# Expert gate and up by halves in three passes, 13 more experts' weights loaded ahead, and the orders at the start and at a seam, in a two-layer transformer kernel

## The chip, the core and the metric

The kernel runs on one core of a Trainium2 chip. A core has TensorE (PE in the profile: matrix products; PEld is its weight load, which overlaps the products), VectorE (DVE), ScalarE (ACT), GpSimd (POOL) and SyncE (SP, which here only issues transfers); 16 DMA engines move data between the chip's memory and the core's on-chip memory. The metric is device time in microseconds (us) of one execution; lower is better. Each engine works through its own list of instructions in order and waits on semaphores where another engine's result is needed.

## The reference, cut to what matters

Two layers act on x of 4 x 256 tokens of width 256 (T = 1024 tokens). All of it is float32.

```
h = layernorm(x) * (1 + ca) + sa                      # layer 0, modulated by a small network on c
x = x + ga * attention0(h)                            # 16 heads, 4-tap causal, gated
h = layernorm(x) * (1 + cb) + sb
x = x + gb * ffn0(h)                                  # silu(h Wg) * (h Wu), Wd; weights decoded from a 16-entry table
h = layernorm(x) * (1 + ca) + sa                      # layer 1
x = x + ga * attention1(h)                            # 16 heads, softmax, mxfp4 weights
h = layernorm(x) * (1 + cb) + sb
x = x + gb * (h + routed(rmsnorm(h)) + shared(rmsnorm(h)))
# routed: each token picks 4 of 32 experts; an expert holds up to 256 tokens:
#   g, u = split(rows @ w13[e]);  rows_out = (silu(g) * u) @ w2[e]
```

## The kernel before

**Layout.** x_t and h_t hold the activations transposed: 128 partitions, two chunks (KC = 2) of 1024 token columns. `psum` is eight banks of 512 float32 columns. `arena` is one large on-chip tile that the phases carve up anew, and `G` another (16 heads x 1024 columns for the attention outputs, then the decoded feed-forward weights). The r forms (`arena_r`, `G_r`) are the same bytes in the type fp32r: a value is rounded to that type when it is written.

**Two ways of multiplying.** A plain float32 product takes two matmul instructions in the trace. The other way is by_halves (lines 641 to 646): each operand is kept as a rounded upper half and the remainder as a lower half, both fp32r, and three matmuls (lower x upper, upper x lower, upper x upper) add into one bank. ACT writes the upper half by a copy, and DVE the lower half by subtracting the upper from the source. Before the change the q, k, z, v projections of layer 0 and the scores and most projections of layer 1 go by halves; the experts do not.

**Start.** The first layernorm runs in two halves of 512 columns, n0a and n0b: mean on PE (L286), subtraction on DVE (L309), squares on ACT (L304), variance on PE (L293), a small TENSOR_SCALAR on DVE (L313), the power -1/2 on POOL (L318), a diagonal of it on DVE (L323), its spreading over partitions by a matmul (L299), then scaling (L329) and modulation (L335) on DVE. The first part of the modulation (`modulation`, PE L622, DVE L1388 and L1393) gives the factors of L335. ACT copies h_t to its upper half (L1224), DVE subtracts (L1419), and the first q projection (L644) waits for that.

**Seam of the two halves of layer 0.** After the heads, PE adds up the output projection (`project_out`, L687: 2 halves n of the tokens x 2 chunks m x 16 heads, one product each), while ACT and DVE decode the feed-forward weights from the table in 13 pieces (`lut_act` L1145 and L1149, `lut_dve` L1487 and L1499). The heads' mean square (r0) comes back from the chip's memory; DVE turns it into a diagonal (L1614), PE spreads it (`spread_pe`, L273), ACT copies it out (L1232), and `attn_half` on DVE (L1583, then L400) uses it. Then come the second norm (n1a, n1b) and the feed-forward (`gate_up` L816, `down` L825). A gate or up product of 512 columns needs a free psum bank: `ffn_bank`.

**Experts.** Before them PE does the layer-1 output projection, DVE the routing (lines 1770 to 1831), and POOL scatters the token rows to `slot_rows` in the chip's memory (32 indirect transfers, L2001). SP loads them back per expert into a ring of 6 (xb, L574), and the weights of an expert (768 columns: 512 of gate and up, 256 of down) into a ring of 4 (L570, then L601). For expert e, PE turns the rows (`turn_rows`, L1041, 4 transposes into bank e % 2), multiplies by gate and up (`up_e`, L1052, 4 products of 256 columns) and by down (`down_e`, L1062). ACT (even e) or DVE (odd e) copies the turned rows out (L1353, L1861), ACT takes silu of the gate (L1359), DVE multiplies with up (L1868), and DVE (even e) or ACT (odd e) copies the output to eo (L1892, L1373). POOL scatters it to `out_rows` by two indirect transfers (L2009), whose targets DVE has copied out (place, L1854). The order is written out by hand: in round e PE does turn_rows(e+2), up_e(e+1), down_e(e). At the end the four chosen rows of each token are read back, weighted and added (o4, in G).

Semaphores of layer 0 are used again in the experts (`REUSED`), so that waits show the old names: a0_q is moe_T, a0_S moe_up_1, a0_A moe_act, a0_vT moe_down, a0_g and a0_gT moe_eo.

## Time and profile before

| what | value |
|---|---|
| median of 3 runs | 1089.62 us (1087.21 to 1091.27) |
| the profiled execution, its own time | 1090.9 us, span on the core 1089.1 us |
| busy share of the span | PE 93%, PEld 74%, DVE 69%, ACT 51%, POOL 26% |
| mean granted TensorE clock | 0.959 |
| start, up to the first q projection | 0 to 27.4 us |
| experts, first turned row to last product | 963.2 to 1062.5 us |

The page gives one row per engine group with its busy time, the mean of one and the idle time before it. The chain of waits follows the work that ended last back from the end; its pieces are laid end to end, so that a piece of eight matmuls divided by eight is the pace of one. The timeline has the same instructions with their full duration: a matmul there shows its own latency, longer than its pace. The granted clock is 1.00 at TensorE's 2.4 GHz level and 0.50 at 1.2 GHz.

### The profile page before, as it was taken

To read this page: it belongs to the slowest core of one execution; us is meant where nothing else is said; L and a number is where in the kernel's file an instruction comes from. 1 tells how busy PE (TensorE), PEld (TensorE's weight loads), DVE (VectorE), ACT (ScalarE), POOL (GpSimd) and SP (SyncE) were. 2 spreads that over 40 slices of the span, in tenths; PEclk is the share of its full clock that TensorE was granted. 3 is DMA by queue.
4 is the path that set the end of the run, shared out by engine and by line. 5 is a ranking of instruction groups with operands and counts; after the bars stand their busy time and mean duration, and the time that the engine had idled before them with its cause. 6 is when DMAs were issued, how large, how long until landed. Compare 5 with 4: busy or idle time off the path is not lost.

```text
span 1089.1 us, 16889 instructions
## 1 busy us (share of the span) xinstructions
PE 1009.2 (93%) x5736; PEld 802.2 (74%) x5736; DVE 751.7 (69%) x1305; ACT 557.8 (51%) x1105; POOL 284.8 (26%) x246
## 2 busy tenths in 40 slices
PE   6979999999999999999979999999996997669996
PEld 4778998898899854354459989889895455358885
DVE  4778999899989859972377777878775144624434
ACT  2558878787887787721155555655552022113231
POOL 1034324423432410030112122121200005436661
PEclk9989999999999999989989999999998998689997
DMA  7087867877876950340011110111002002169956
GB/s 225 3 217 153 190 147 161 169 171 157 166 159 158 259 110 19 133 109 0 1 59 51 37 58 29 58 44 43 29 0 73 0 1 87 57 201 272 274 180 207
DMA packets 82477, 121.56 MB, mean 112 GB/s; under 512 B 26099, under 2 KB 59646, under 8 KB 81792
## 3 DMA queue, kind: packets, MB, share of 16 engines
q1 hardware_dynamic: 70400, 86.88, 26.8%
q0 software_dynamic: 12032, 34.11, 15.9%
q8 instruction: 25, 0.41, 0.2%
q14 instruction: 20, 0.16, 0.0%
HBM read 70.28 MB, written 38.04 MB: 99 GB/s over the span
## 4 chain that ended last, share of the span: by engine, by line
PE 79%; DVE 11%; DMA 3%; ACT 3%; issue 3%; POOL 1%; SPq 0%; ACTq 0%; DVEq 0%; POOLq 0%
PE psum L644 10%; PE psum L646 9%; PE psum L645 9%; PE psum L1052 5%; PE psum L869 5%; PE psum L698 5%; PE psum L1011 5%; PE psum L816 4%; PE psum L894 3%; PE psum L776 3%; PE psum L757 3%; PE psum L1062 2%; PE psum L687 2%; PE psum L825 2%; DVE arena L1511 2%
## 5 line engine op out<-in xcount | busy, mean ns | idle before, releaser
L1511 DVE SCALAR_TENSOR_TENSOR arena<-arena,par_in 128x1024 f32<-128x1024 f32 x144 | 183.5, 1283 | 32.8 <-ACT arena L1136 23.2
L644 PE MATMUL psum<-G_r,arena_r 128*128 128x512 f32 x320 | 132.6, 414 | 7.2 <-DVE G_r L1604 4.1
L645 PE MATMUL psum<-G_r,arena_r 128*128 128x512 f32 x320 | 127.5, 399 | 0.0
L646 PE MATMUL psum<-G_r,arena_r 128*128 128x512 f32 x320 | 127.4, 398 | 0.0
L1960 POOL DMA_DIRECT2D arena<-arena x64 | 53.8, 984 | 210.8 <-DVE arena L1523 210.6
L1284 ACT ACTIVATE arena<-psum,small 128x256 f32<-128x256 f32 x128 | 59.4, 474 | 86.9 <-DVE small L1669 86.9
L1126 ACT ACTIVATE arena<-psum 128x1024 f32<-128x1024 f32 x48 | 49.3, 1027 | 62.2 <-PE psum L646 61.6
L644 PE MATMUL psum<-arena_r 128*128 128x256 f32 x256 | 77.7, 304 | 2.2 <-DVE arena_r L1694 1.5
L644 PEld LDWEIGHTS psum<-G_r,arena_r 128*128 128x128 f32 x320 | 61.2, 191 | 21.2 <-DVE G_r L1604 4.9
L1976 POOL TENSOR_TENSOR arena_r<-arena,arena_r 128x512 fp32r<-128x512 f32 x16 | 20.7, 1294 | 214.2 <-ACT arena_r L1253 214.2
L2009 POOL DMA_INDIRECT out_rows<-arena x64 | 62.6, 979 | 46.8 <-DVE arena L1854 24.5
L645 PE MATMUL psum<-arena_r 128*128 128x256 f32 x256 | 73.4, 287 | 0.0
L646 PE MATMUL psum<-arena_r 128*128 128x256 f32 x256 | 73.3, 286 | 0.0
L646 PEld LDWEIGHTS psum<-G_r,arena_r 128*128 128x128 f32 x320 | 60.8, 190 | 14.8
L645 PEld LDWEIGHTS psum<-G_r,arena_r 128*128 128x128 f32 x320 | 61.3, 192 | 11.4 <-issue 0.2
L2001 POOL DMA_INDIRECT slot_rows<-arena x32 | 31.3, 980 | 128.1 <-issue 111.7
L698 PE MATMUL psum<-cst,arena 128*128 128x128 f32 x512 | 63.9, 278 | 0.0
L869 PE MATMUL psum<-arena,h_t 128*128 128x128 f32 x512 | 62.3, 275 | 0.0
L698 PEld LDWEIGHTS psum<-cst,arena 128*128 128x128 f32 x512 | 59.7, 191 | 3.4 <-issue 3.3
L869 PEld LDWEIGHTS psum<-arena,h_t 128*128 128x128 f32 x512 | 60.9, 192 | 1.5
L1052 PE MATMUL psum<-arena 128*128 128x256 f32 x256 | 61.7, 385 | 0.0
L1136 ACT ACTIVATE arena<-arena,par_in 128x1024 f32<-128x1024 f32 x48 | 55.4, 1154 | 5.5
(243 smaller groups left out, 2375.3 us busy)
## 6 DMA issues: line engine op xcount, KB each, us to landing
arena<-arena POOLq DMA_DIRECT2D x64, 256.0 KB, 5.7
arena<-in_w_moe SPq DMA_DIRECT2D x33, 384.0 KB, 3.9
slot_rows<-nowhere SPq DMA_DIRECT2D x16, 576.0 KB, 4.4
arena<-slot_rows SPq DMA_DIRECT2D x32, 288.0 KB, 4.1
arena<-bands SPq DMA_DIRECT2D x16, 528.0 KB, 4.2
sq_rows<-arena POOLq DMA_DIRECT2D x16, 512.0 KB, 7.5
arena<-in_w_qkvz SPq DMA_DIRECT2D x16, 384.0 KB, 3.8
arena<-in_qkv_codes SPq DMA_DIRECT2D x16, 384.0 KB, 3.2
```

The source lines that it names most:

```text
L644: nc.tensor.matmul(dst, w_l, x_h, start=start, stop=False, skip_group_check=True)
L645: nc.tensor.matmul(dst, w_h, x_l, start=False, stop=False, skip_group_check=True)
L646: return nc.tensor.matmul(dst, w_h, x_h, start=False, stop=stop, skip_group_check=True)
L698: m = nc.tensor.matmul(bank(7)[:, n:n + P], sqr[s][:, i * P:i * P + P], ones, start=True, stop=True, skip_group_check=True)
L869: i = nc.tensor.matmul(dst[:, t * P:t * P + P], h_t[:, k * T + t * P:k * T + t * P + P], w1[par][:, (2 * KC + k) * P:(2 * KC + k) * P + P] ...
L1011: i = nc.tensor.matmul(bank(2 * m + n), wo_c[:, h * D + m * P:h * D + m * P + P], G[:, (OS + h) * T + n * 512:(OS + h) * T + n * 512 + 512 ...
L1052: i = nc.tensor.matmul(bank(2 + 2 * (e % 2) + j)[:, 0:CAP], we[e % WRING][:, k * D + j * P:k * D + j * P + P], xT[e % 2][:, k * CAP:(k + 1 ...
L1136: nc.scalar.activation(by_batch(dst), by_batch(u[s])[:, :, 0:S], ACT.Copy, scale=par_in[:, bass.ds(M_CW + (w * H + h) * TAPS, 1)]).then_in ...
L1284: e = nc.scalar.activation(prob[b % 2][:, i * S:i * S + S], bank(4 + b % 2)[:, i * S:i * S + S], ACT.Exp, bias=nmax[:, 2 * b + i:2 * b + i ...
L1511: nc.vector.scalar_tensor_tensor(by_batch(dst), by_batch(u[s])[:, :, j:j + S], par_in[:, bass.ds(M_CW + (w * H + h) * TAPS + j, 1)], by_ba ...
L1960: nc.gpsimd.dma_start(rot[s][to:to + 64, :], sw[s][of:of + 64, :], accum_op=ALU.add)\
L2009: nc.gpsimd.indirect_dma_start(out_rows, bass.IndirectOffsetOnAxis(place.bitcast(I32)[:, c:c + 1], 0), eo[e % RING][:, r * D:(r + 1) * D], ...
```

## The change

**Experts.** Gate and up go by halves. The turned rows of every expert are copied by ACT to an upper half x_h and subtracted by DVE to a lower half x_l; the gate and up weights likewise to w_h and w_l (2 buffers each). So ACT makes 2 copies of 128x512 per expert where it made one for every other expert, and DVE 2 subtractions of 128x512 where it made one copy for every other expert. PE waits in up_e for w_lo and x_lo. `down_e` stays as it is.

**Weights.** After all of layer 1's output projection has been added up, SP loads experts 4 to 16 at once into the tile G that held the attention outputs. Only 15 experts (17 to 31) are loaded inside the rounds, by the table LATE.

**Start.** PE does the variances before the first modulation; DVE does the split of the first weights (lower0) before the first diagonal, and scales the second half and splits the first before it modulates the second half.

**Seam.** PE spreads r0 five products later. The gate and up of the second piece of the first half (n, m) = (0, 1) go to banks 6 and 7, so that the wait for attn_half(1) moves from that piece (s == 1) to s == 3.

```diff
+AHEAD = 13
+LATE = {1: 27, 3: 28, 5: 29, 7: 17, 8: 18, 10: 19, 11: 20, 13: 21, 14: 22, 16: 23, 17: 24, 19: 25, 20: 26, 22: 30, 24: 31}
...
+        e_halves = carve(*[2 * CAP] * 4, *[2 * D] * 4, base=at_x + NT * TOPK + 2 * E, of=arena_r)
+        x_h, x_l, w_h, w_l = e_halves[0:2], e_halves[2:4], e_halves[4:6], e_halves[6:8]
...
+        w_ahead = carve_g(EW + 4 * T, *[EW] * AHEAD)
...
+            return e - 10 if e < 27 else e - 27
...
-        def ffn_bank(m, up):
+        def ffn_bank(n, m, up):
-            return bank(((0, 3), (1, 2))[m % 2][up])
+            return bank((6, 7)[up] if (n, m) == (0, 1) else ((0, 3), (1, 2))[m % 2][up])
...
+            sp.wait_ge(sg("attn_out"), 4 * KC)
+            for e in range(WRING, WRING + AHEAD):
+                sp.dma_start(we_of(e), a["w_moe"][e]).then_inc(sg("moe_ahead"), 16)
...
-                    if e + WRING < E:
-                        sp.wait_ge(*at("moe_down", e + 1))
-                        sp.dma_start(we[e % WRING], a["w_moe"][e + WRING]).then_inc(sg(f"moe_w{e % WRING}"), 16)
+                    if e in LATE:
+                        late, r = LATE[e], LATE_NTH[LATE[e]] % WRING
+                        sp.wait_ge(*at("moe_down", before(late) + 1))
+                        sp.wait_ge(sg(f"moe_w{r}"), 16 * (LATE_NTH[late] // WRING + 1))
+                        sp.dma_start(we_of(late), a["w_moe"][late]).then_inc(sg(f"moe_w{r}"), 16)
...
-            spread_pe(pe, "r0", fb)
...
-            project_out(1, 0, range(0, 5))
+            project_out(1, 0, range(0, 2))
+            spread_pe(pe, "r0", fb)
+            project_out(1, 0, range(2, 5))
...
-                    if s == 1:
+                    if s == 3:
                         pe.wait_ge(sg("y"), KC + up + 1)
...
             def up_e(e):
-                pe.wait_ge(*at(f"moe_w{e % WRING}", 16 * (e // WRING + 1)))
-                pe.wait_ge(*at(f"moe_xT_{e % 2}", e // 2 + 1))
+                pe.wait_ge(*at("moe_w_lo", e + 1))
+                pe.wait_ge(*at("moe_x_lo", e + 1))
...
-                        i = nc.tensor.matmul(bank(2 + 2 * (e % 2) + j)[:, 0:CAP],
-                                             we[e % WRING][:, k * D + j * P:k * D + j * P + P],
-                                             xT[e % 2][:, k * CAP:(k + 1) * CAP], start=(k == 0), stop=(k == KC - 1))
+                        w, c = slice(k * D + j * P, k * D + j * P + P), slice(k * CAP, (k + 1) * CAP)
+                        i = by_halves(bank(2 + 2 * (e % 2) + j)[:, 0:CAP], w_h[e % 2][:, w], w_l[e % 2][:, w],
+                                      x_h[e % 2][:, c], x_l[e % 2][:, c], k == 0, k == KC - 1)
...
+            def weights_e(e):
+                act.wait_ge(*weights_in(e))
+                if e >= 2:
+                    act.wait_ge(*at("moe_up_1", e - 1))
+                nc.scalar.activation(w_h[e % 2], we_of(e)[:, 0:2 * D], ACT.Copy).then_inc(sg("moe_w_hi"), 1)
...
+            weights_e(0)
+            weights_e(1)
             rows_e(0)
+            rows_e(1)
             silu_e(0)
             for e in range(E):
-                if e % 2 == 0 and e + 2 < E:
+                if e + 2 < E:
                     rows_e(e + 2)
+                    weights_e(e + 2)
...
-                nc.vector.tensor_copy(xT[1], bank(1)).then_inc(sg("moe_xT_1"), 1)
+                nc.vector.tensor_tensor(x_l[e % 2], bank(e % 2), x_h[e % 2].bitcast(F32), ALU.subtract).then_inc(sg("moe_x_lo"), 1)
+
+            def weights_e(e):
+                dve.wait_ge(*at("moe_w_hi", e + 1))
+                if e >= 2:
+                    dve.wait_ge(*at("moe_up_1", e - 1))
+                nc.vector.tensor_tensor(w_l[e % 2], we_of(e)[:, 0:2 * D], w_h[e % 2].bitcast(F32), ALU.subtract)\
+                    .then_inc(sg("moe_w_lo"), 1)
...
                 if e + 2 < E:
+                    rows_e(e + 2)
+                    weights_e(e + 2)
                     place_e(e + 2)
-                if e % 2 and e + 2 < E:
-                    rows_e(e + 2)
```

The list of DVE from its first subtraction, before (L313 the statistic, L323 the diagonal, L1413 lower0, L329 scaling, L335 modulation, L1388 and L1393 the first modulation):

```order
4 L309 TENSOR_TENSOR arena<-x_t,psum 128x512
5 L1388 COPY small<-psum 128x16 [waits mod_ps]
6 L1393 TENSOR_SCALAR small<-small 128x8 [waits mod]
7 L313 TENSOR_SCALAR small<-psum 128x4 [waits norm_var,mod]
8 L323 TENSOR_TENSOR arena<-cst,small 128x512 [waits norm_rstd]
9 L313 TENSOR_SCALAR small<-psum 128x4 [waits norm_var]
10 L323 TENSOR_TENSOR arena<-cst,small 128x512 [waits norm_rstd]
11 L1413 TENSOR_TENSOR arena_r<-arena,arena_r 128x768 [waits a0_w_hi]
12 L329 TENSOR_TENSOR arena<-arena,psum 128x512 [waits norm_spread]
```

The same stretch of DVE after the change (L342 is the statistic, L1464 lower0, L352 the diagonal, L358 scaling, L1439 and L1444 the modulation):

```order
4 L338 TENSOR_TENSOR arena<-x_t,psum 128x512
5 L342 TENSOR_SCALAR small<-psum 128x4 [waits norm_var]
6 L1464 TENSOR_TENSOR arena_r<-arena,arena_r 128x768 [waits a0_w_hi]
7 L352 TENSOR_TENSOR arena<-cst,small 128x512 [waits norm_rstd]
8 L342 TENSOR_SCALAR small<-psum 128x4 [waits norm_var]
9 L352 TENSOR_TENSOR arena<-cst,small 128x512 [waits norm_rstd]
10 L358 TENSOR_TENSOR arena<-arena,psum 128x512 [waits norm_spread]
11 L358 TENSOR_TENSOR arena<-arena,psum 128x512
12 L1439 COPY small<-psum 128x16 [waits mod_ps]
```

The statistic no longer stands behind the modulation, and lower0 stands where DVE waits for POOL's power.

PE at the seam, before (L687 output projection, L273 the spread of r0, L342 the mean of n1a):

```order
626 L687 MATMUL psum<-G,arena 128x512 [waits a0_v_tok]
627 L687 MATMUL psum<-G,arena 128x512 x13
628 L273 MATMUL psum<-arena,cst 128x512 [waits norm_diag,a0_gT_sb]
629 L273 MATMUL psum<-arena,cst 128x512
630 L687 MATMUL psum<-G,arena 128x512 x3
631 L687 MATMUL psum<-G,arena 128x512 [waits a0_on]
632 L687 MATMUL psum<-G,arena 128x512 x4
633 L342 MATMUL psum<-x_t,cst 128x512 [waits x_new] x2
```

PE at the seam after the change (L727, L302 and L377 are the same three):

```order
628 L727 MATMUL psum<-G,arena 128x512 x13
629 L727 MATMUL psum<-G,arena 128x512 [waits a0_gT_sb]
630 L727 MATMUL psum<-G,arena 128x512 x2
631 L727 MATMUL psum<-G,arena 128x512 [waits a0_on]
632 L727 MATMUL psum<-G,arena 128x512
633 L302 MATMUL psum<-arena,cst 128x512 [waits norm_diag]
634 L302 MATMUL psum<-arena,cst 128x512
635 L727 MATMUL psum<-G,arena 128x512 x3
636 L377 MATMUL psum<-x_t,cst 128x512 [waits x_new] x2
```

Five products now stand ahead of the wait for the diagonal (norm_diag).

DVE in two rounds of the experts, before (L1854 place, L1861 turned rows, L1868 silu times up, L1892 output copy):

```order
748 L1854 COPY arena<-arena 128x2 [waits moe_xb0]
749 L1868 TENSOR_TENSOR arena<-psum,arena 128x256 [waits a0_vT,a0_o,a0_S]
750 L1892 COPY arena<-psum 128x512 [waits moe_sc4,moe_over0,a0_vT]
751 L1854 COPY arena<-arena 128x2 [waits moe_xb1]
752 L1861 COPY arena<-psum 128x512 [waits a0_S,a0_q]
753 L1868 TENSOR_TENSOR arena<-psum,arena 128x256 [waits a0_vT,a0_o,a0_S]
```

DVE in two rounds after the change (L1914 is x_lo, which waits for a0_k = moe_x_hi; L1920 w_lo, which waits for a0_ssq = moe_w_hi; L1907, L1928, L1948, L1955 are place, product, one of eight additions of y0 to x_t, output copy):

```order
734 L1914 TENSOR_TENSOR arena_r<-psum,arena_r 128x512 [waits a0_S,a0_k]
735 L1920 TENSOR_TENSOR arena_r<-G,arena_r 128x512 [waits a0_S,a0_ssq]
736 L1907 COPY arena<-arena 128x2 [waits moe_xb4]
737 L1928 TENSOR_TENSOR arena<-psum,arena 128x256 [waits a0_vT,a0_o,a0_S]
738 L1948 SCALAR_TENSOR_TENSOR x_t<-G,small,x_t 128x256
739 L1955 COPY arena<-psum 128x512 [waits moe_sc2,moe_over0,a0_vT]
740 L1914 TENSOR_TENSOR arena_r<-psum,arena_r 128x512 [waits a0_S,a0_k]
741 L1920 TENSOR_TENSOR arena_r<-G,arena_r 128x512 [waits a0_S,a0_ssq]
```

Every round now begins with two subtractions of 128x512, each behind a copy of ACT. On PE a round has 12 fp32r matmuls of 256 columns (L684 to L686) where 4 float32 products stood (L1052, 8 instructions in the trace), between the same transposes and the same down products.

## Rows read from the trace of the kernel before

**Rows 1.** The page: busy time, share and instructions of each engine.

```profile
PE 1009.2 (93%) x5736; PEld 802.2 (74%) x5736; DVE 751.7 (69%) x1305; ACT 557.8 (51%) x1105; POOL 284.8 (26%) x246
```

**Rows 2.** Chain of waits, one expert round: start, us, engine and line.

```profile
986.29 0.44 PE psum L1041 x4
986.73 1.73 PE psum L1052 x8
988.46 0.86 PE psum L1062 x4
```

**Rows 3.** Chain, layer 1: the pace of fp32r matmuls of 256 columns.

```profile
667.39 0.12 PE psum L644
667.51 0.12 PE psum L645
```

**Rows 4.** Windows: PE, PEld, DVE, ACT, POOL busy (count), clock, DMA share, GB/s.

```profile
910.00:920.00 10.00, 5.96 (x33) 4.93 (x31) 3.53 (x8) 2.84 (x6) 7.56 (x9) 0.80 0.31 112
983.00:1003.00 20.00, 20.00 (x108) 17.63 (x107) 10.83 (x28) 5.78 (x13) 13.00 (x13) 1.00 0.90 268
```

**Rows 5.** Timeline, one expert round, ACT and DVE: start, duration, instruction, idle before.

```profile
986.82 0.59 ACT L1353 ACTIVATE arena<-psum 128x512 f32<-128x512 f32 x1
987.63 0.38 ACT L1359 ACTIVATE arena<-psum 128x256 f32<-128x256 f32 x1 [0.22 <-PE psum L1052]
988.50 0.42 DVE L1868 TENSOR_TENSOR arena<-psum,arena 128x256 f32<-128x256 f32 x1 [2.13 <-PE psum L1052]
989.36 0.69 DVE L1892 COPY arena<-psum 128x512 f32<-128x512 f32 x1
```

**Rows 6.** Timeline, POOL's scatters beside a DVE instruction with two on-chip inputs.

```profile
997.93 0.97 POOL L2009 DMA_INDIRECT out_rows<-arena  x1 [1.71 <-issue]
999.20 0.98 POOL L2009 DMA_INDIRECT out_rows<-arena  x1 [0.30 <-ACT arena L1373]
...
997.92 0.48 DVE L1885 SCALAR_TENSOR_TENSOR x_t<-G,small,x_t 128x256 f32<-128x256 f32 x1
```

**Rows 7.** Chain of waits at the start, up to the first q projection.

```profile
12.58 1.68 PE psum L622 x16
14.26 1.90 PE psum L293 x16
...
16.58 1.05 POOL small L318
...
17.66 0.69 DVE arena L323
...
20.24 0.87 DVE arena_r L1413
21.11 1.20 DVE arena L329 x2
22.31 1.29 DVE h_t L335 x4
...
26.08 1.21 DVE G_r L1419 x2
...
27.43 0.77 PE psum L644
```

**Rows 8.** Window inside the first q projection, same columns as rows 4.

```profile
30.00:31.00 1.00, 1.00 (x4) 0.71 (x4) 0.00 (x0) 0.00 (x0) 0.00 (x0) 0.50 0.00 0
```

**Rows 9.** Timeline at the seam: PE, ACT and DVE.

```profile
415.41 1.96 PE L273 MATMUL psum<-arena,cst 128*128 128x512 f32 x4 [2.19 <-DVE arena L1614]
...
457.91 3.70 PE L816 MATMUL psum<-h_t,G 128*128 128x512 f32 x8 [1.59 <-DVE arena L1583]
...
434.64 0.16 DVE L313 TENSOR_SCALAR small<-psum 128x4 f32<-128x4 f32 x1 [2.08 <-PE psum L293]
...
430.80 4.00 ACT L1145 ACTIVATE arena<-arena,small 128x336 f32<-128x336 int32 x7
```

**Rows 10.** Timeline: a DVE product while POOL multiplies a long tile.

```profile
476.06 8.59 DVE L323 TENSOR_TENSOR arena<-cst,small 128x512 f32<-128x512 f32 x1
```

67 lines of the change are left out of this document (46 added, 21 removed).

## The prediction

> **What bounds the kernel now.** I read the page's busy line first: PE is busy for 93% of the span and no other engine comes near [rows 1], so time is won where PE's own work shrinks or where PE stands waiting. Then I read the chain of waits, in order of time, at the places that the change touches. In the experts a round on the chain consists of PE alone: 0.44 us of transposes, 1.73 us of gate and up, 0.86 us of down, 3.03 us in all [rows 2]. PE has no gap there (20.00 of 20.00 us), while in 20 us DVE works 10.83 us, ACT 5.78, POOL 13.00; the next nearest limit is the DMA engines, with a share of 0.90 [rows 4]. At the start the chain is a relay of short steps that ends in DVE work, and PE starts the first q projection at 27.43 us [rows 7]. At the seam PE waits twice, 2.19 us for the diagonal of r0 and 1.59 us for a free bank [rows 9].
>
> **Experts, gate and up.** Eight float32 instructions take 1.73 us, 0.216 each [rows 2]. By halves there are 2 x 2 x 3 = 12 fp32r matmuls of the same 256 columns. Layer 1 runs that very form at a pace of 0.12 us [rows 3], so 12 take 1.44 us. A round saves 1.73 - 1.44 = 0.29 us and takes 2.74. There are 31 rounds at the full clock, so 31 x 0.29 = 9.0 us, if PE stays the limit.
>
> The row says that one fp32r pass costs 0.12 and a float32 product 0.43, a ratio of 3.6. The Trainium skill (FP8 and Floating Point Precision, TensorE Precision Notes) has a true FP32 product as 4 passes, by which three passes would take 1.73 x 3/4 = 1.30 us and save 0.43 a round, 13.4 us in all; this is a rival below, and the sum goes by the row.
>
> Does PE stay the limit at 2.74 us? ACT per round: x_h, priced by the present copy of turned rows at 0.59, w_h of the same size at about the same, silu 0.38, and an output copy every other round at 0.6 / 2 = 0.3 [rows 5]: 1.9 us. DVE: x_lo and w_lo at 1.21 / 2 = 0.6 each, the price of the same 128x512 subtraction at the start [rows 7], the product 0.42, half an output copy 0.35 [rows 5], the small place copy under 0.2: 2.2 us, in eight rounds 0.48 more for an addition of y0 [rows 6]. Both fit into 2.74. The latency has to fit too. PE cannot start up(e+1) before w_lo(e+1), which stands behind turn(e+1), x_h, w_h and x_lo. From the end of up(e-1): down 0.86, transposes 0.44, some 0.2 for the signal, x_h 0.6, w_h 0.6, 0.1, w_lo 0.6, then up(e+1) itself 1.44: 4.8 us, against two rounds, 5.5. The loop has 0.6 us to spare, so I put the conversions at nothing; the cover is gone once they grow by more than 0.6 us.
>
> POOL needs two scatters a round, 0.97 us each with 0.30 between [rows 6], so 2.54 us when it has them in stock: under 2.74, but close. On SP the waits for turned rows and place come later in a round, since place now stands behind two subtractions; behind them queue the late weights and the overflow row, and the rows so loaded are needed six rounds later. I put that at nothing. The conversions of the first two weights lie in the wait for the first rows, where ACT and DVE have nothing else. The first round gets longer by x_lo, 0.6 us, before up(0), partly paid back by the shorter up(0): I take 0.2 us lost. Experts together: 8.8 us, bounds 6 (a third of the gain lost to the loop or to POOL) and 9.2.
>
> **Weights ahead.** A round moves today 384 KB of weights and the rows in and out at a DMA share of 0.90 in 3.03 us [rows 4]. Squeezed into 2.74 us that would be 0.90 x 3.03 / 2.74 = 0.995, no reserve. With 15 instead of 28 experts loaded inside the rounds this falls: 268 GB/s x 3.03 us is 812 KB a round; without the weights 419; the mean of the new kernel is 419 + 393 x 15 / 32 = 603 KB, in 2.74 us 220 GB/s, a share of about 0.74. The 13 loads are 5.1 MB, issued once the output projection is done, while POOL makes its first scatters. POOL's first scatters run beside them at a share of 0.31 and 112 GB/s [rows 4]; at the 268 GB/s shown the loads take 19 us, and the window of the scatters lies some 50 us ahead of the first round at 963, so nothing is late. So the loads themselves cost nothing, and they buy the room for the shorter round.
>
> **Start.** Before, 16 instructions of the modulation (1.68 us) stand ahead of the variance, L1413 (0.87) stands between the second diagonal and the scaling, and the modulation of the second half (1.29) ahead of the split L1419 [rows 7]. New order from 12.58 us, by the same durations: variance of n0a 1.90, statistic and signals 0.4, POOL 1.05, to 15.9; lower0 has to wait for ACT's copy at 15.4 and so ends at 16.3; diagonal 0.69, to 17.0; second statistic, POOL and diagonal 2.1, to 19.1; scaling 1.20; modulation's small steps 0.5; L335 1.29; scaling of n0b 1.2, which hides ACT's copies; split 1.21; to 24.5, and PE at 24.65. The gain is 27.43 - 24.65 = 2.8 us. Before, the first products then run at a granted clock of 0.50, the 1.2 GHz level [rows 8], after PE had stood waiting for the split. In the new order PE comes straight from the second modulation. If the clock stays up, the 12 products save up to 1.1 us more, until the second split sets their end. Between 0 and 1.1 I take 0.4: 3.2 us in all, bounds 1.0 (lower0 delaying the diagonal more than worked out) and 3.9. What follows is a chain through DVE, bands and weight transfers which are all issued relative to it, so it moves as a whole.
>
> **Seam.** The five products moved ahead of the spread take 5 x 2 x 0.43 = 4.3 us (512 columns, twice 0.216) where PE waited 2.19 [rows 9], so the spread comes 2.1 us later, ACT copies it later, and DVE gets it about 1 us later. DVE is in the table decode, yet idles 2.08 us before L313 [rows 9], which covers that. PE gains what of its wait isn't turned into a wait for x_new, about 0.9 us at that L313; but ACT's decode piece of 4.00 us [rows 9] then comes 0.8 later and DVE waits for it, which leaves about 0.2. The bank change takes away the wait of 1.59 us, but then s == 3 waits for a product which DVE does behind a decode piece; there I count 0.5. Together 0.7 us, bounds -1.0 (a loss, if the later spread delays the decode) and 3.8 (both waits gone).
>
> **Sum.** 8.8 + 3.2 + 0.7 = 12.7 us. The profiled execution took 1090.9 us, so its like would take 1078.2; it lay 1.3 above the median of 1089.6, so I forecast 1076.9 us.
>
> **Rivals.**
> (a) Conversions pace the rounds. The loop has 0.6 us to spare in two rounds. Against it: ACT is busy in 5.78 of 20 us now [rows 4]. If the loop grows so far that a round stays at 3.03, only start and seam remain: 3.9 us, 1085.7.
> (b) Four passes against three. If fp32r matmuls had a pace of 1.30 / 12 = 0.108 us, the sum would be 13.4 + 3.9 - 0.2 = 17.1 us, 1072.5. Against it stands the pace of 0.12 in rows 3; this is what the Trainium skill's count of passes, named above, comes to.
> (c) Slower: VectorE and GpSimd block each other. Once, a DVE product of this size took 8.59 us while POOL multiplied a long tile [rows 10]; elsewhere it takes 0.69 [rows 7]. The new kernel puts two 128x512 subtractions into each round, and POOL's scatters run in two thirds of it. If each subtraction waited for a whole scatter, DVE's round would be 2.2 + 2 x 0.97 = 4.1 us, and 31 x (4.1 - 3.03) = 34 us would be lost, less 3.9: 1120. It decides from waits of 0.95 us a round (2.2 + 0.95 = 3.15, where 31 x 0.12 eats the 3.9). Against it: a DVE instruction with two on-chip inputs starting together with a scatter took 0.48, and the scatter 0.97 [rows 6], as they do apart.
> The Trainium skill (SBUF — State Buffer, Who interferes with whom) says that a DVE instruction with two SBUF inputs contends with a GpSimd instruction that reads SBUF, the second to issue blocking fully; w_lo is such an instruction, x_lo with its psum input is not. The trace agrees for the long multiplication and shows no block by a scatter.
> (d) The earlier start is swallowed by a transfer that doesn't move: 12.7 - 3.2 = 9.5 us, 1080.1.
>
> **How the numbers follow.** The forecast has 0.78, (a) 0.10, (b) 0.04, (c) 0.04, (d) 0.04. The bounds of the terms sum to gains of 6.0 and 16.9 us, 1083.6 and 1072.7; I set the range to 1072.5 to 1084.5, which leaves out (a) at its full size and (c). About 0.5%, or 5.4 us, is what a measurement can tell from no change: faster means under 1084.2. The forecast, (b) and (d) lie there: 0.86. Same holds (a): 0.10. Slower is (c): 0.04.
>
> **What would show it.** In the new chain a round should be 2.74 us with 12 fp32r matmuls at 0.12 and no idle on PE; a wait of PE for w_lo or x_lo would show (a). DVE's w_lo should last 0.6 to 0.7 us, a spread up to 1.6 would show (c). The DMA share in the rounds should fall to about 0.75. PE's first q product should start near 24.7 us, and PE's wait at the r0 spread should be gone, with a wait for x_new of 1 to 2 us behind it. The forecast is wrong if POOL falls behind (gaps of 0.30 throughout and scatters ending many us after the last product), or if the clock, back at 0.50 in some stretch, takes from PE what the passes gave.

## The result, and the profile after

The changed kernel takes 1077.12 us in the median of 4 runs (1075.58 to 1078.86), the kernel before 1090.3 (1087.21 to 1091.27): a ratio of 0.9896, 95% interval 0.9875 to 0.9918. Another set, further down, gives 0.9900 (0.9876 to 0.9924). The forecast was 1076.9 us, a ratio of 0.988. The profiled execution took 1078.86 us, its span 1077.0, 12.1 us shorter than the 1089.1 of before; the sum forecast 12.7. The total is right, but under it the first round, the end of the kernel and the start are not what the sum said.

**The rounds** came out as forecast. Chain of waits of the changed kernel, one expert round, columns as in [rows 2]:

```profile
1041.26 0.44 PE psum L1082 x4
1041.69 0.12 PE psum L684
1041.81 0.12 PE psum L685
1041.93 0.12 PE psum L686
...
1043.00 0.12 PE psum L686
1043.12 0.86 PE psum L1103 x4
1043.98 0.44 PE psum L1082 x4
```

From one first transpose to the next it is 2.72 us (12 products of 0.12 between 0.44 and 0.86) where [rows 2] had 3.03. PE waits nowhere in the windows, which answer to [rows 4] (same columns):

```profile
910.00:920.00 10.00, 7.80 (x40) 7.57 (x40) 3.16 (x10) 3.33 (x6) 5.59 (x6) 0.66 0.91 363
983.00:1003.00 20.00, 20.00 (x147) 18.77 (x146) 17.54 (x42) 11.38 (x25) 14.72 (x15) 1.00 0.84 257
1003.00:1023.00 20.00, 20.00 (x150) 18.92 (x149) 14.44 (x33) 12.04 (x26) 15.38 (x15) 1.00 0.82 248
```

PE works 20.00 of 20.00 us; DVE rose from 10.83 to 17.54 and ACT from 5.78 to 11.38. The DMA share is 0.82 to 0.84 in these two windows against 0.90. The loads ahead run at 363 GB/s beside POOL's first scatters. ACT, DVE and POOL in a round, timeline of the changed kernel, columns as in [rows 5]:

```profile
987.54 0.97 POOL L2072 DMA_INDIRECT out_rows<-arena  x1 [0.30 <-ACT arena L1424]
988.49 0.68 DVE L1920 TENSOR_TENSOR arena_r<-G,arena_r 128x512 fp32r<-128x512 f32 x1
988.82 1.20 POOL L2072 DMA_INDIRECT out_rows<-arena  x1 [0.30 <-issue]
...
989.92 0.60 ACT L1394 ACTIVATE arena_r<-psum 128x512 fp32r<-128x512 f32 x1 [1.28 <-PE psum L1082]
990.42 0.62 ACT L1400 ACTIVATE arena_r<-G 128x512 fp32r<-128x512 f32 x1
990.55 0.69 DVE L1914 TENSOR_TENSOR arena_r<-psum,arena_r 128x512 fp32r<-128x512 f32 x1
```

w_lo (L1920) takes 0.68 us, x_lo (L1914) 0.69, the copies on ACT 0.60 and 0.62.

**The first round** is another matter. Timeline of PE at the first turned rows:

```profile
958.01 1.94 PE L1082 MATMUL psum<-cst,arena 128*128 128x128 f32 x8 [10.40 <-DMA arena<-slot_rows]
960.60 0.55 PE L684 MATMUL psum<-arena_r 128*128 128x256 f32 x1 [0.65 <-DVE arena_r L1914]
...
966.61 1.03 PE L1103 MATMUL psum<-arena 128*128 128x256 f32 x4
```

From the first transpose to the first down product it takes 8.60 us; before, the same piece ran from 963.18 to 970.12, 6.94 us. The new kernel waits 0.65 us for x_lo and runs at a granted clock of 0.50, the 1.2 GHz level, longer: the windows 962 to 964 and 964 to 966 still show 0.50 and 966 to 968 shows 0.88, 8 us and more after its first transpose, while before it was back at 1.00 from 968 on, 5 us after. It is not this profile alone: the piece takes 8.2 to 8.6 us in the eight profiles with gate and up by halves and nothing added ahead of the rows, and 6.9 to 7.4 in the four with float32 experts.

**The start.** Chain of the changed kernel, which answers to [rows 7], and windows that answer to [rows 8]:

```profile
14.95 0.96 DVE arena_r L1464
15.91 0.61 DVE arena L352
16.52 0.04 issue
16.57 1.13 PE psum L328 x2
17.69 1.68 PE psum L662 x16
19.37 0.96 PE psum L328 x2
20.34 5.92 PE psum L662 x32
26.26 0.63 PE psum L684
```

```profile
20.00:21.00 1.00, 1.00 (x10) 0.82 (x8) 1.00 (x4) 0.30 (x1) 0.00 (x0) 0.99 1.08 176
21.00:22.00 1.00, 1.00 (x7) 1.00 (x7) 1.00 (x3) 0.96 (x2) 0.00 (x0) 0.50 0.26 52
```

DVE's relay went a little better than worked out (its split of the first half ends at 23.7 us, 24.5 in the forecast), but it no longer ends the start: PE does, with the second modulation. These 32 narrow matmuls take 5.92 us, because the granted clock falls to 0.50 while PE works through them. The first q product starts at 26.12, not at 24.65. In `f32_ahead` (experiment 8), whose start is the same, the clock stays at 1.00 through them, and q starts at 23.16. PE's timeline there:

```profile
19.48 3.63 PE L663 MATMUL psum<-small,G 128*128 128x4 f32 x32
```

**What came without being forecast.** The load of the third head's weights decides when PE goes on at 60 us (chain; first line before, second line after):

```profile
54.08 8.65 DMA arena<-in_w_qkvz
```

```profile
52.78 5.91 DMA arena<-in_w_qkvz
```

It starts 1.3 us and ends 4.0 us earlier, and PE waits 2.56 us instead of 5.51. A long wait costs once more behind itself, by the clock. Windows before and after, columns as in [rows 4]:

```profile
60.00:70.00 10.00, 5.44 (x27) 5.44 (x28) 5.16 (x5) 5.97 (x7) 1.85 (x1) 0.66 1.04 267
```

```profile
60.00:70.00 10.00, 9.47 (x67) 9.39 (x68) 8.71 (x8) 8.85 (x16) 0.77 (x1) 0.83 1.06 284
```

In `start_only` (experiment 2) the same window has 1.00. What that is worth stands below the table of landmarks.

**The seam.** PE's timeline of the changed kernel, which answers to [rows 9]:

```profile
412.90 1.88 PE L302 MATMUL psum<-arena,cst 128*128 128x512 f32 x4
...
418.13 1.98 PE L377 MATMUL psum<-x_t,cst 128*128 128x512 f32 x4 [0.78 <-DVE x_t L435]
...
460.51 3.70 PE L857 MATMUL psum<-h_t,G 128*128 128x512 f32 x8 [0.94 <-DVE arena L1651]
```

PE no longer waits for the diagonal (2.19 us before). It waits 0.78 us for x_new, where 1 to 2 was forecast, and 0.94 us at s == 3 for a product that DVE makes (L1651), where it waited 1.59 for the bank.

### The profile page after: what moved, and what is told of

Read it like the earlier page. It is cut to its first block, busy times and chain, and to the rows that moved or that the text cites. A ratio compares the mean times of both kernels' runs of the same rounds, so it can differ in the third digit from the quotient of the medians.

```text
span 1077.0 us, 17346 instructions
## 1 busy us (share of the span) xinstructions
PE 1004.1 (93%) x5864; PEld 802.5 (75%) x5864; DVE 779.0 (72%) x1353; ACT 580.7 (54%) x1153; POOL 287.7 (27%) x246
## 4 chain that ended last, share of the span: by engine, by line
PE 78%; DVE 12%; ACT 4%; issue 3%; DMA 2%; POOL 1%; SPq 0%; ACTq 0%; DVEq 0%; POOLq 0%
PE psum L684 11%; PE psum L686 11%; PE psum L685 11%; PE psum L910 5%; PE psum L738 5%; PE psum L1052 5%; PE psum L935 3%; PE psum L727 3%; PE psum L816 3%; PE psum L857 3%; PE psum L797 3%; PE psum L1103 2%; PE psum L866 2%; DVE arena L1564 2%; PE psum L820 1%
## 5 line engine op out<-in xcount | busy, mean ns | idle before, releaser
L1564 DVE SCALAR_TENSOR_TENSOR arena<-arena,par_in 128x1024 f32<-128x1024 f32 x144 | 183.4, 1282 | 33.4 <-ACT arena L1177 23.7
L684 PE MATMUL psum<-G_r,arena_r 128*128 128x512 f32 x320 | 132.8, 415 | 4.6 <-DVE G_r L1657 4.1
L686 PE MATMUL psum<-G_r,arena_r 128*128 128x512 f32 x320 | 127.8, 399 | 0.0
L684 PE MATMUL psum<-arena_r 128*128 128x256 f32 x384 | 117.8, 307 | 2.9 <-DVE arena_r L1747 1.5
L685 PE MATMUL psum<-arena_r 128*128 128x256 f32 x384 | 110.8, 288 | 0.0
L686 PE MATMUL psum<-arena_r 128*128 128x256 f32 x384 | 110.8, 288 | 0.0
L684 PEld LDWEIGHTS psum<-arena_r 128*128 128x128 f32 x384 | 75.7, 197 | 3.8 <-issue 2.7
L2039 POOL TENSOR_TENSOR arena_r<-arena,arena_r 128x512 fp32r<-128x512 f32 x16 | 20.7, 1294 | 214.7 <-ACT arena_r L1294 214.7
L685 PEld LDWEIGHTS psum<-arena_r 128*128 128x128 f32 x384 | 75.9, 198 | 0.0
L2072 POOL DMA_INDIRECT out_rows<-arena x64 | 65.9, 1029 | 36.9 <-DVE arena L1955 19.3
L686 PEld LDWEIGHTS psum<-arena_r 128*128 128x128 f32 x384 | 75.7, 197 | 0.0
L684 PEld LDWEIGHTS psum<-G_r,arena_r 128*128 128x128 f32 x320 | 61.5, 192 | 18.7 <-DVE G_r L1657 4.9
L686 PEld LDWEIGHTS psum<-G_r,arena_r 128*128 128x128 f32 x320 | 61.0, 191 | 14.8
```

The lines of the kernel that those rows point to most:

```text
L684: nc.tensor.matmul(dst, w_l, x_h, start=start, stop=False, skip_group_check=True)
L685: nc.tensor.matmul(dst, w_h, x_l, start=False, stop=False, skip_group_check=True)
L686: return nc.tensor.matmul(dst, w_h, x_h, start=False, stop=stop, skip_group_check=True)
L1564: nc.vector.scalar_tensor_tensor(by_batch(dst), by_batch(u[s])[:, :, j:j + S], par_in[:, bass.ds(M_CW + (w * H + h) * TAPS + j, 1)], by_ba ...
L2072: nc.gpsimd.indirect_dma_start(out_rows, bass.IndirectOffsetOnAxis(place.bitcast(I32)[:, c:c + 1], 0), eo[e % RING][:, r * D:(r + 1) * D], ...
```

## The experiments

Landmarks, in us of the span, each read from PE's timeline in the profiled execution: the first q product; PE going on behind that weight load; the 16 products (L776 before, L816 after) of the last head but one, at the end of the heads' loop; the wait for a diagonal ahead of layer 1's projections (the third spread); the first turned rows of the experts; the table products behind the last round (L1083 before, L1124 after); the end. "c" is the granted clock in the window 475 to 495; "again" is the changed kernel profiled a second time (9).

```
            q     PE on  heads   layer 1  rows    tables    end     c
before      27.43 64.56  373.00  546.09   963.18  1068.97  1089.1  0.83
exp_only    27.65 64.40  373.06  546.59   963.59  1061.22  1082.0  0.83
seam_only   27.27 63.22  372.01  542.48   959.35  1065.24  1085.3  0.91
start_only  26.14 60.44  367.51  541.95   959.01  1065.12  1085.5  0.74
after       26.12 60.52  368.24  540.66   958.01  1055.98  1077.0  0.83
again       26.03 61.44  369.04  541.26   958.25  1055.81  1076.6  0.83
ring4       26.11 60.51  367.57  541.58   959.10  1067.12  1088.0  0.74
mod_late    23.16 61.89  370.45  543.04   960.65  1058.55  1079.3  0.83
fill_late   23.47 60.77  374.76  546.66   963.96  1062.16  1083.1  0.83
warm        26.09 62.39  370.09  542.12   959.55  1054.54  1075.2  0.83
dbl_w       23.38 59.72  367.39  539.63   957.98  1065.98  1086.7  0.83
beside      25.98 62.32  370.01  539.36   956.77  1054.55  1075.4  1.00
best        26.13 63.25  372.28  541.15   958.47  1053.56  1074.4  1.00
f32_ahead   23.16 59.67  367.39  537.55   954.41  1060.12  1080.3  0.91
```

Such a table is worth more here than the medians: a kernel's runs spread over 3 to 12 us, while rows to tables takes 97.97, 97.56 and 97.63 us in `after`, `again` and `exp_only`, whose experts are the same. Part of the spread goes with the clock: the 12 runs of `dbl_w` have a mean granted clock from 0.956 (1093.36 us) to 0.962 (1081.49 us), the 6 of `beside` from 0.955 (1082.41) to 0.963 (1070.26).

From PE going on to the heads' end it takes 308.4 to 308.8 us in the three profiles with the old start. With the new one it takes 307.1 in the two where the clock stays at 1.00 behind the wait (`start_only`, `ring4`), 307.6 to 307.7 in six where it is at 0.50 for about 3 us, and 308.6 and 309.0 in `mod_late` and `best`, where it is at 0.50 for as long as with the old start. (`fill_late` is held up in this stretch by its own edit.) In the mean the start has gained 3.0 us where PE goes on and 3.9 at the heads' end (without `mod_late` and `fill_late`).

**1. The experts' part alone.** `exp_only` is the changed kernel with the diffs of 2 and 3 undone.

> The experts' part alone (gate and up by halves, 13 weights ahead), start and seam as before. Theory: PE paces the rounds at 2.74 us, so the gain is the 7.4 us that the two traces show between the first turned row and the last down product, less 0.9 in the tail: 6.5 us, up to the 8.8 of the prediction, so a ratio of 0.992 to 0.994. Rival: the forecast's other parts were worth nothing and the experts gave all 12: 0.989.

1081.19 us (4 runs), ratio 0.9925 (0.9897 to 0.9952), 8.1 us, as expected. Rows to tables 97.63 us against 105.79, 8.2 us. The experts carry two thirds of the gain. The 12 us rival falls.

**2. The start alone.**

```diff
+            part_var_pe(pe, "n0a", n0_sq[0], 5)
+            part_var_pe(pe, "n0b", n0_sq[1], 7)
+            part_spread_pe(pe, "n0a", n0_d[0], 4)
             pe.wait_ge(sg("silu_c"), 2)
             pe.wait_ge(sg("in_wmod0"), 16)
             modulation(0, 3, (SA, CA))
-            part_var_pe(pe, "n0a", n0_sq[0], 5)
-            part_var_pe(pe, "n0b", n0_sq[1], 7)
-            part_spread_pe(pe, "n0a", n0_d[0], 4)
```

(and the order of DVE that goes with it.)

> The start's order alone. Theory A (the later weight load is shorter by nature of the new order): 1.1 us from the first q product at 26.1 instead of 27.4, and 3 us more because the load of the third head's weights takes 5.9 us instead of 8.7: 4.1 us, ratio 0.996. Theory B (that load's length is chance): 1.1 us, ratio 0.999, and loads of 5.9 and of 8.7 us in runs of either kernel. The prediction said 3.2 us, all of it before the first q product.

1087.28 us (10 runs), ratio 0.9980 (0.9959 to 1.0002). PE goes on at 60.44, 4.1 us earlier, and the load takes 5.84 us; at the heads' end it is 5.5 us ahead. By 546 us 1.4 of that is gone: the clock window there shows 0.74 instead of 0.83. The median is 2.0 us under that of the kernel before, with an interval that includes no change and the ratio of either theory, so the medians don't decide between A and B. As to the load, see 5 and 9.

**3. The seam alone.**

```diff
+            return bank((6, 7)[up] if (n, m) == (0, 1) else ((0, 3), (1, 2))[m % 2][up])
...
-            project_out(1, 0, range(0, 5))
+            project_out(1, 0, range(0, 2))
+            spread_pe(pe, "r0", fb)
+            project_out(1, 0, range(2, 5))
...
-                    if s == 1:
+                    if s == 3:
```

> The seam alone (spread of r0 later, gate and up of piece (0,1) in banks 6 and 7). The prediction: 0.7 us, bounds -1.0 and 3.8. From the two traces: 1.0 us, since the changed kernel is 4.4 us ahead at 404 us and 5.4 at 500. Rival: the waits only move, 0.0.

1087.31 us (10 runs), ratio 0.9985 (0.9965 to 1.0006): 2.0 us by the medians, and the interval includes no change. From the heads' end to layer 1 it takes 170.47 us against 173.09, 2.6 us, but its clock window is 0.91. A window of 20 us at a mean clock c has lost 20 x (1 - c): 3.4 us at 0.83, 5.2 at 0.74, 1.8 at 0.91. With that taken off, the stretch is 169.7, 170.1 and 169.2 us in the three kernels with the old seam, and 168.7 here and 168.4 to 169.4 in the ten others with the new one, 168.8 in the mean: the seam is worth 0.9 us. In the profiles parts 1 to 3 add up to 14.5 us of the span where the whole has 12.1. Of the 2.4 between them, 1.7 are there at the heads' end already, ahead of the seam (5.5 and 1.0 us gained in `start_only` and `seam_only`, 4.8 in the whole): that is the weight load and the clock behind it, see 9. How the 0.9 divides between the later spread and the banks was not tried.

**4. By halves without the loads ahead.**

```diff
-AHEAD = 13
-LATE = {1: 27, 3: 28, 5: 29, 7: 17, 8: 18, 10: 19, 11: 20, 13: 21, 14: 22, 16: 23, 17: 24, 19: 25, 20: 26, 22: 30, 24: 31}
+AHEAD = 0
+LATE = {e: e + 4 for e in range(28)}
...
-            return e - 10 if e < 27 else e - 27
+            return e - WRING
```

> The changed kernel with no expert loaded ahead: all 28 later experts through the ring of four, each load issued once the down product four experts before is done. Theory of the prediction: 0.90 x 3.03 / 2.74 = a DMA share of 0.995 to 1.0, so the rounds stretch from 2.74 towards 2.9 to 3.0 and 5 to 8 us are lost against the changed kernel (1082 to 1085). Rival: the transfers still fit, the rounds stay at 2.74 and the time at 1077.

1087.6 us (10 runs), ratio 0.9989 (0.9969 to 1.0010): some 10 us over the changed kernel. Rows to tables take 108.0 us, longer than before. Windows and PE's timeline of this kernel:

```profile
985.00:1005.00 20.00, 18.65 (x132) 16.84 (x131) 15.03 (x34) 10.88 (x23) 12.69 (x14) 1.00 0.84 254
```

```profile
996.36 0.39 PE L684 MATMUL psum<-arena_r 128*128 128x256 f32 x1 [0.76 <-DVE arena_r L1920]
```

PE waits for w_lo, behind which stands a load (4.1 to 5.2 us on the chain). The loss is larger than expected, and the reason is another: the DMA share is 0.84, not 1. DVE and SP's queue in the same round, timeline of `ring4`:

```profile
995.61 0.69 DVE L1920 TENSOR_TENSOR arena_r<-arena,arena_r 128x512 fp32r<-128x512 f32 x1 [1.15 <-ACT arena_r L1400]
996.22 0.16 DVE L1907 COPY arena<-arena 128x2 int32<-128x2 int32 x1
...
996.46 0.38 SPq L612 DMA_DIRECT2D arena<-slot_rows  x1
996.93 0.42 SPq L641 DMA_DIRECT2D arena<-in_w_moe  x1
```

The load of expert e+4 (L641) stands on SP behind the wait for place(e+2), and place (L1907) now stands on DVE behind w_lo(e+2), which needs the load of expert e+2. So each load waits for the one before the last, by way of two conversions: 4.1 to 5.2 us of load, 0.64, 0.70, 0.16 for place, 0.48 to issue the rows, 6.1 to 7.2 us, for two rounds of 5.45. SP stands 23 times at the wait for place, 31.6 us in all, and 5 times at that for the down product four experts before (5.7 us). Before the change it stood 27 times at the down product (32.5 us) and once at place. The changed kernel waits for place as well (21 times, 20.4 us), but nothing that stands behind it is needed soon. Place ahead of the two subtractions was not tried.

**5. The start's two open points.** In `mod_late` the second modulation is moved on PE behind the first q projection, to the second head; in `fill_late` the clears behind that weight load are moved to the end of the loop.

```diff
-            modulation(0, 2, (GA, SB_, CB, GB))
...
+                if is_last(h, 1):
+                    modulation(0, 5, (GA, SB_, CB, GB))
```

> The changed kernel, with the second modulation (32 matmuls of 128x4, 6.1 us on PE at the clock of 0.50 ahead of the first q product) moved on PE to the second head, ahead of its z projection where PE waits 2.6 us, into bank 5; DVE's part of it follows behind that head's k convolution. Theory (PE itself set the start's end): the first q product starts at 23.8 to 24.0 instead of 26.1, the q projection ends 2.3 us earlier (29.3), and 3.6 us of matmuls against a wait of 2.6 give back 1.0: 1.3 us net, 1075.8. Rival (DVE's split or the first weights set the end): q at 26 as before and the time 1.0 us longer, 1078.1.

The q product starts at 23.16 us, 3 us earlier: PE was the last. But PE goes on at 61.89, since the load, issued at 49.23, took 10.83 us. 1081.94 us (6 runs), ratio 0.9920 (0.9892 to 0.9948), 3.4 and 4.8 us over the two medians of the changed kernel, with intervals that overlap. In this profile PE goes on 1.4 us behind it, is 2.2 us behind at the heads' end, the other 0.8 by the clock behind the wait, and 2.3 at the end.

```diff
+                if not is_last(h, 0):
+                    fill(h)
+                if is_last(h, H - 2):
+                    fill(0)
```

(`fill(h)` holds the two clearing transfers of a head.)

> The changed kernel, with the first head's two clearing transfers (slot_rows and out_rows, 832 KB, issued right behind the weight load of the third head) issued after the last but one head instead. Theory (that load, 5.9 us long, shares the DMA engines with the clears): the load takes 3.5 to 4.5 us, PE's wait of 2.56 us at 57.6 us shrinks to about 1 or less, 1.5 to 2.5 us gained: 1075.1. Rival (the load waits for something else, such as the gates' four moves on POOL's queue): 5.9 us still, 1077.1.

1084.44 us (12 runs), ratio 0.9963 (0.9943 to 0.9984). The load still took 8.98 us with no clear behind it, against 8.30 and 8.53 in `dbl_w` and `f32_ahead`, whose q starts as early and whose clears are in place; so by this one profile the clears don't stretch it. Neither the theory nor the rival came true. The moved clears are issued at 328 and 330 us; PE then stands for 4.39 us up to 347.61, for which the profile names no releaser, the clock falls behind it, and PE is 6.5 us later at 374.76. What does share the load's stretch are POOL's four moves of 256 KB, and from 58 to 61 us the DMA share is about 1 (0.95 to 1.2) in every kernel. That they stretch the load wasn't tried.

**6. The first rounds' clock.** `warm` puts 10 matmuls that nobody reads into the wait for the first rows.

```diff
             pe.wait_ge(*at("moe_wov_sb", 1))
+            for _ in range(10):
+                nc.tensor.matmul(bank(7), ident, x_t[:, 0:512], start=True, stop=True)
             turn_rows(0)
```

> The changed kernel, with 10 float32 matmuls of 128x512 into bank 7 whose result nobody reads, in PE's wait of 10.4 us ahead of the first turned rows. Theory (the first rounds lose 1.8 us because the granted clock is 0.50 up to 966.6 after that wait): the clock stays at 1.00 from 958 on, the first two rounds take 2.7 to 3 us, 1.5 to 1.9 us gained: 1075.4. Rival: the clock falls all the same, or the dummies end after the rows' arrival: 0 to 0.5 lost.

Windows of the changed kernel and of `warm`:

```profile
958.00:962.00 4.00, 3.34 (x14) 2.97 (x15) 1.52 (x4) 1.20 (x2) 0.00 (x0) 0.50 1.03 353
```

```profile
958.00:962.00 4.00, 2.39 (x12) 1.16 (x11) 1.17 (x3) 1.19 (x2) 0.00 (x0) 1.00 0.97 287
```

The clock stays at 1.00, and rows to tables take 94.99 us against 97.97: 3.0 us. The median does not show it, 1078.22 us (5 runs), ratio 0.9897 (0.9880 to 0.9915); `best` below does.

**7. How much the conversions have to spare.**

```diff
+                nc.scalar.activation(G[:, 15200 + e % 2 * 512:15712 + e % 2 * 512], we_of(e)[:, 0:2 * D], ACT.Copy)
                 nc.scalar.activation(w_h[e % 2], we_of(e)[:, 0:2 * D], ACT.Copy).then_inc(sg("moe_w_hi"), 1)
...
+                nc.vector.tensor_tensor(arena_r[:, 23280 + e % 2 * 512:23792 + e % 2 * 512], we_of(e)[:, 0:2 * D], w_h[e % 2].bitcast(F32), ALU.subtract)
```

> The changed kernel, with the copy of the weights' upper half on ACT and the subtraction of their lower half on DVE done twice per expert, the first time into columns that nobody reads. Prediction: the loop of two rounds has 0.6 us to spare; 0.6 + 0.6 = 1.2 to 1.3 us more exceed it by 0.6 to 0.7, so a round takes 3.05 to 3.1 instead of 2.74 and 31 rounds lose 10 us: 1087. If DVE's own load decides (2.2 + 0.6 + the additions: 2.9 to 3.4 in the rounds with an addition of y0), it is like that or a little more, up to 1090. Rival (the loop has far more to spare than worked out): rounds of 2.74 and 1077.

PE's timeline of `dbl_w`:

```profile
1031.58 0.39 PE L684 MATMUL psum<-arena_r 128*128 128x256 f32 x1 [0.21 <-DVE arena_r L1922]
...
1037.68 0.38 PE L684 MATMUL psum<-arena_r 128*128 128x256 f32 x1 [0.20 <-DVE arena_r L1922]
```

Two rounds take 6.10 us, 3.05 each; 1088.35 us (12 runs), ratio 0.9980 (0.9959 to 1.0001). Two rounds were 5.45 and grew by 0.65 for about 1.2 us more work in the loop, so the loop had 0.5 to 0.6 us to spare, as worked out. DVE is busy for 17.45 of 20 us from 1023 to 1043 there, so its own load is not what sets the 3.05.

**8. The loads ahead without the halves.** `f32_ahead` has gate and up in float32 again, the turned rows copied by ACT alone.

```diff
-                        i = by_halves(bank(2 + 2 * (e % 2) + j)[:, 0:CAP], w_h[e % 2][:, w], w_l[e % 2][:, w],
-                                      x_h[e % 2][:, c], x_l[e % 2][:, c], k == 0, k == KC - 1)
+                        i = nc.tensor.matmul(bank(2 + 2 * (e % 2) + j)[:, 0:CAP], we_of(e)[:, w], x_f[e % 2][:, c],
+                                             start=(k == 0), stop=(k == KC - 1))
```

> The changed kernel with gate and up in float32 again (8 instructions of 0.216 a round, turned rows copied by ACT alone, no halves of the weights), but 13 experts' weights ahead as in the change. Theory (the loads ahead buy nothing by themselves, they make room for the shorter round): rounds of 3.03 us at a DMA share of 0.65 to 0.75, so 31 x 0.29 = 9 us over the changed kernel: 1086. Rival (the loads within the rounds cost time already before): rounds under 3.03 and a time under 1084.

1086.70 us (12 runs), ratio 0.9973 (0.9956 to 0.9990). One round on its chain, and a window:

```profile
986.56 0.44 PE psum L1083 x4
987.00 1.73 PE psum L1095 x8
988.73 0.86 PE psum L1104 x4
```

```profile
983.00:1003.00 20.00, 20.00 (x108) 17.65 (x107) 7.28 (x22) 8.43 (x17) 12.85 (x14) 1.00 0.78 231
```

Rounds of 3.03 us at a share of 0.78, and 105.71 us from rows to tables against 105.79: the loads ahead alone buy nothing. Halves alone cost 2, loads alone give 0, both together give 8.

**9. The changed kernel again, and layer 1's modulation dealt out.**

> The changed kernel itself, unaltered, once more beside the three others of this set. Theory A (the start's length is decided by when the granted clock falls, which differs between executions of the same order): 1077 to 1079 in the median, and in this profile the first q product at either 23.4 (clock up during the second modulation, 3.63 us) or 26.1 (clock at 0.50, 5.6 to 6.1 us). Theory B (the small edits of the kernels in which it began at 23.4 did it): again 26.1.

1078.54 us (6 runs), ratio 0.9900 (0.9876 to 0.9924); the first q product at 26.03. Over all profiles with the new start and the modulation in its place it began at 26.0 to 26.1 in seven and at 23.2 to 23.5 in three (`dbl_w`, `fill_late`, `f32_ahead`), whose edits all act later than this place. In those three the modulation took 3.63 us at a clock of 1.00. The weight load took 5.8 to 6.4 us in four of the ten and 8.3 to 9.0 in six; with the old start 7.5 to 8.7 in three. This run by itself fits both theories, with q at 26.03. For A speak the three, since nothing in them differs up to that place, and the mean clock, which differs between the runs of one kernel (above); but no single kernel was profiled with both starts of q. For the load there is a third possibility: the runs were made on two chips, and with the new start the load took 5.84 us in both profiles known to be of the first (`start_only`, `ring4`) and 6.37 to 8.98 in the seven of the second. Execution and chip are not told apart here.

```diff
-            modulation(1, 5, range(6))
+            pe.wait_ge(sg("lut_done"), LCH)
...
+            down(0, range(0, 4), beside)
             part_spread_pe(pe, "n1b", fb)
-            pe.wait_ge(sg("lut_done"), LCH)
-            down(0)
+            down(0, range(4, MT))
```

(`beside` issues one or two of the twelve pairs of the modulation behind each product.)

> The changed kernel, with layer 1's modulation (48 instructions of 128x4, 5.75 us in one piece at 473) dealt out between the first eight down products of 128x512 of the first half. Theory (the clock falls after that long piece of narrow matmuls and costs half of what is done until it rises, 3.4 us in the window 475 to 495 whose mean clock is 0.83): the clock stays at 1.00 there, 3.4 us gained: 1074. Rival (the clock falls for another reason, or the later spread makes PE wait for DVE): 0 to 2 lost.

Windows of the changed kernel and of `beside`:

```profile
475.00:495.00 20.00, 19.79 (x63) 10.42 (x63) 9.53 (x22) 0.00 (x0) 3.58 (x1) 0.83 0.00 1
```

```profile
475.00:495.00 20.00, 20.00 (x82) 11.38 (x81) 11.78 (x23) 0.58 (x1) 5.25 (x1) 1.00 0.00 1
```

The clock stays at 1.00 (0.83 in the changed kernel), and from PE's gate and up at 462.77 to the layer 1 landmark at 539.36 it takes 76.59 us against 80.15 (460.51 to 540.66): 3.6 us. The median of 6 runs is 1077.06, ratio 0.9881 (0.9849 to 0.9914); alone it can't be told from the changed kernel's.

**10. Both together.** `best` has the edits of `warm` and `beside`.

> The changed kernel with both stretches of half clock worked on: layer 1's modulation dealt out between down products, and 10 unread matmuls of 128x512 in the wait ahead of the experts' first rows. Theory: 3.4 + 3.0 (from the first turned rows to the table products 95.0 us with those matmuls against 98.0 without) = 6.4 us, 1071 to 1072. Rival (what is gained at a stretch is lost again in the next wait for a transfer): 1077.

1071.06 us (6 runs, 1067.52 to 1076.34), ratio 0.9828 (0.9802 to 0.9855), against 0.9900 (0.9876 to 0.9924) of the changed kernel in the same set: 7.5 us faster than that, 6.4 expected. Its own profile is of a slow one of its runs (1076.25 us, with PE on at 63.25), yet ends 2.6 us ahead.

## Why the prediction was right, step by step

- **A round of 2.74 us, PE the limit.** Right: 12 products at 0.12, no wait on PE. The slack held, 0.5 to 0.6 us (`dbl_w`), so rival (a) falls. Rival (b) falls by the pace of 0.12. The Trainium skill (FP8 and Floating Point Precision, TensorE Precision Notes) counts a true FP32 product as 4 passes; here the ratio of a float32 product to one fp32r matmul is 1.73 / 1.44 x 3 = 3.6, and the measurement decides.
- **The first round: mis-sized.** 0.2 us was taken, 1.7 measured (8.60 against 6.94), since only x_lo's wait was counted and not that the work between the rows and the first down product runs at the clock of 0.50, and that this level lasts longer behind the new order. With those 10 unread matmuls ahead of the rows, which keep the clock at 1.00, the same piece takes 5.5 us (`warm`, `best`). Why the level lasts longer stays open. The rest of the rounds gave 9.1 us, and the step from the last down product to the table products is 0.4 shorter, which nothing forecast. So the experts gave 7.8 us up to the table products (105.79 against 97.97), not 8.8.
- **The tail: left out.** From the table products to the end it takes 21.0 us instead of 20.1. On the chain PE works through it without a wait in both kernels (first line before, second after):

```profile
1076.12 9.19 PE psum L1094 x64
```

```profile
1063.14 10.10 PE psum L1135 x64
```

  The 0.9 us is the clock: it is at 0.50 for 11.0 us from the first table product before the change, and for 12.9 after it, and the products of those 1.9 us run at half the pace. The tail is 20.1 to 20.4 us in the four profiles with float32 experts and 20.7 to 21.0 in the ten with halves; why the level lasts longer behind them stays open. POOL is not the reason. It was called close in the prediction, and it is: 57 of its 64 scatters begin 0.30 or 0.31 us behind the one before, and the last ends 7.2 us behind the last down product instead of 6.4. But in `ring4` and `dbl_w` the last scatter ends 1.0 us ahead of the table products, as before the change, and the tail is 20.9 and 20.7 us all the same.
- **Weights ahead.** Right that they are free and needed (`f32_ahead`, `ring4`). The share was worked out as 0.74, a mean over all 32 rounds; it is 0.82 to 0.88 from 983 to 1033 us and 0.30 from there to 1043, since the 15 late loads all lie in the first 25 rounds. That without them a share of 0.995 would be the limit was the wrong reason: the loop from load to load through place is, at a share of 0.84. That SP's wait for place comes later was seen and put at nothing; with the loads ahead it costs nothing, without them it costs all that the halves gain.
- **The start: wrong step, nearly the right sum.** The working took PE as ready and let DVE's split set the start of q. PE's second modulation sets it, at 26.1 us with the clock at 0.50; with the modulation out of the way q starts at 23.2. It starts there too with the modulation in its place where the clock stays at 1.00 (23.2 to 23.5 in three profiles); so the step that failed is that PE's own work, at a clock that can fall while it works, was put at nothing. The gain at q was 1.3 us instead of 2.8 plus 0.4. What followed was said to move as a whole; it does not. PE goes on behind the weight load at 64.1 us in the mean of three profiles with the old start, at 61.1 in the mean of ten with the new one: 3.0 us, against 3.2 forecast. Part of the start is swallowed by a transfer, which is rival (d) in part: the three profiles with q 2.7 us earlier go on only 1.5 us earlier (60.05 against 61.55). In the profile shown here the load was short, by 2.7 us, which the new order doesn't ensure. That 3.0 comes near 3.2 is luck: it is a short q gain and a load that varies by more than both. The clock behind that wait gives another 0.9 us by the heads' end, which no term of the sum has.
- **The seam.** 0.7 forecast, 0.9 measured once the clock is taken off. The waits moved as said, in smaller sizes (0.78 us for x_new, 0.94 at s == 3).
- **Rival (c)** did not come: w_lo took 0.68 us. There is a trace of it the other way round: the scatters' mean is 1029 ns where it was 979, 1051 in `dbl_w` and 978 in `f32_ahead`. It follows the subtractions. The Trainium skill (SBUF — State Buffer, Who interferes with whom) says that a DVE instruction with two SBUF inputs contends with a GpSimd instruction that reads SBUF; here it is 0.1 to 0.23 us on some scatters and nothing on DVE.

Together: 7.8 - 0.9 + 3.0 + 0.9 (clock behind the load) + 0.9 (seam) = 11.7 us, against 11.0 and 13.2 by the medians and 12.1 in the profiled pair, which had luck with one load. The mechanism of the largest term was right; that the total came so near is in part luck, since what was missing (1.5 in the first round, 0.9 in the tail, 1.9 at q) was largely made up by gains that nothing forecast (1.7 up to where PE goes on, 0.9 by the clock behind it, 0.4 ahead of the table products).

## What to carry to other kernels

A change that shortens a round needs its supply looked at in the same step, by the time from one load to the next and not by the DMA share, and with every wait that stands ahead of the load in the issuing engine's list: either half of this change alone gives nothing. Where a relay between engines is rearranged, add up each engine's own work at its possible lower clock too, since the one that waited before may be last after. And where a kernel's runs differ by more than the effect, measure the length of a stretch between two landmarks, with the granted clock beside it; once the clock is taken off, those of the rounds and of the seam repeat here to within 1 us.

## What the runs showed of the hardware

The granted clock of PE fell to 0.50 while PE was working back to back, not only after a wait. Layer 1's modulation in `after` and `start_only`, timeline of PE, and the window of `start_only` over it:

```profile
473.23 5.75 PE L662 MATMUL psum<-small,G 128*128 128x4 f32 x48
```

```profile
473.10 7.85 PE L628 MATMUL psum<-small,G 128*128 128x4 f32 x48
```

```profile
475.00:495.00 20.00, 20.00 (x60) 11.55 (x59) 7.58 (x19) 0.00 (x0) 2.72 (x1) 0.74 0.00 1
```

The same 48 instructions take 5.75 or 7.85 us, and the mean clock behind them is 0.74 to 0.91, depending on the execution; dealt out between wide products they leave it at 1.00 (`beside`, above, and `best`). The Trainium skill (TensorE: Matmul & The Clock Gate, What's actually happening) lists the half rate as that of an idle or cold engine; the trace shows it on an engine with no idle time at all. What exactly the chip weighs is left open. Wide products, dealt out between the narrow ones or put into a wait, kept the clock at 1.00 in both stretches where that was tried.

A weight load of 384 KB issued at the same place took between 5.8 and 10.8 us, with a DMA share of about 1 in its second half. The one profile without the clears behind it speaks against them as the cause (8.98 us); the rest is open.
